# Four-layer block, last layer: part of ScalarE's and VectorE's feature work goes to GpSimd, and 72 expert tiles are spread over 82 blocks

## What is computed

```python
# L3 attention: 16 heads of 64 (1024 columns), a linear attention by features
def _feature_map(t):
    return jax.nn.elu(t) + 1.0
q = jnp.einsum('bsi,ihd->bshd', x, wq) + bq
k = jnp.einsum('bsi,ihd->bshd', x, wk) + bk
v = jnp.einsum('bsi,ihd->bshd', x, wv) + bv
Q = _feature_map(q)
K = _feature_map(k)
KV = jnp.einsum('bshd,bshd->bhd', K, v, precision=HI)
Ksum = jnp.sum(K, axis=1)
Z = 1.0 / (Q * Ksum[:, None, :, :] + EPS)
attn = Q * KV[:, None, :, :] * Z
out = jnp.einsum('bshd,hdo->bso', attn, wo) + bo
return jax.nn.gelu(out)

# L3 experts: the 2 best of 8 per token, hidden width 512
combine = jnp.sum(jax.nn.one_hot(top_idx, E) * routing_weights[..., None], axis=1)
for e in range(E):
    g = x @ gate_w[e].T
    u = x @ up_w[e].T
    y = jax.nn.silu(g) * u @ down_w[e].T
    out = out + combine[:, e:e + 1] * y

# the layer
xn = _layernorm(x, axis=-1)
x = x + _L3_attn_ref(xn, ...) + _L3_ffn_ref(xn, ...)
```

## Time and profile before

| | before |
|---|---|
| device time, median of 3 runs | 2943.32 us |
| span of the profiled execution (first to last instruction) | 2847.3 us |
| its device time beside the span | not listed; the runs shown took 2940.13 to 2945.33 us |
| PE busy over the span | 2442.7 us (86%) |
| DVE busy | 2005.6 us (70%) |
| ACT busy | 1823.8 us (64%) |
| POOL busy | 787.6 us (28%) |
| last layer's tile stage, from 2380.0 us | 332.5 us |
| from there to the first gather of the experts' results | 8.8 us |
| from the first gather (2721.3 us) to the end | 126.0 us |

### The profile page before, as it was taken

The page is one execution under the profiler, slowest core; times in us unless marked ns, Lnnn a source line. Parts: engine busy times, 40 slices in busy tenths (PEclk is TensorE's granted clock), DMA queues, the critical chain, the costliest instruction groups (busy, mean ns, idle before and its releaser), DMA issues. The chain is left out here.

```text
span 2847.3 us, 76648 instructions
## 1 busy us (share of the span) xinstructions
PE 2442.7 (86%) x30232; PEld 1812.5 (64%) x30232; DVE 2005.6 (70%) x5914; ACT 1823.8 (64%) x3779; POOL 787.6 (28%) x820
## 2 busy tenths in 40 slices
PE   6858999996889999999999899989996658999964
PEld 6745677774556666566656665666664547999943
DVE  5556544444568776877687677877775498999988
ACT  3334555553566666666666667666763488999997
POOL 3325100002133232323232223222222163111167
PEclk9959999997999999999999999999999689999998
DMA  6201355551000000000000000000000014666611
GB/s 211 38 16 40 115 158 160 155 156 56 11 17 15 4 17 17 15 4 17 17 15 4 17 17 17 9 10 13 14 13 7 1 45 156 203 195 202 192 42 51
DMA packets 104306, 175.17 MB, mean 62 GB/s; under 512 B 16273, under 2 KB 73745, under 8 KB 103825
## 3 DMA queue, kind: packets, MB, share of 16 engines
q1 hardware_dynamic: 94608, 153.20, 18.0%
q0 software_dynamic: 8192, 16.79, 2.0%
q10 hardware_dynamic: 1152, 0.27, 0.0%
HBM read 130.50 MB, written 26.74 MB: 55 GB/s over the span
## 5 line engine op out<-in xcount | busy, mean ns | idle before, releaser
L2014 POOL TENSOR_TENSOR l_rinv<-l_ssm,w_neg_half 128x8 f32<-128x8 f32 x128 | 210.2, 1642 | 551.8 <-DVE l_ssm L2305 551.7
L257 PE MATMUL bank<-l_kT,l_qT 32*128 32x128 f32 (+1 forms) x3072 | 355.0, 350 | 8.8 <-DVE l_qm L1382 7.2
L257 PE MATMUL bank<-l_qm,l_kT 32*128 32x128 f32 (+1 forms) x3072 | 350.7, 347 | 6.3 <-DVE l_qm L2215 6.3
L2045 ACT ACTIVATE l_probsT<-bank 128x768 f32<-128x768 f32 x256 | 208.5, 815 | 160.1 <-PE bank L257 159.3
L276 DVE TENSOR_REDUCE l_tops<-bank 128x2 f32<-128x256 f32 (+1 forms) x384 | 196.1, 511 | 119.9 <-PE bank L257 116.5
L2717 DVE RECIPROCAL l_rden<-l_den 128x256 f32<-128x256 f32 x128 | 223.8, 1748 | 30.0 <-ACT l_den L2628 29.4
L893 POOL DMA_INDIRECT back<-sorted_y,pos x128 | 125.6, 981 | 378.7 <-DMA sorted_y<-l_y_tile 347.8
L277 DVE TENSOR_REDUCE l_tops<-bank 128x2 f32<-128x512 f32 (+1 forms) x384 | 227.5, 592 | 0.0
L257 PEld LDWEIGHTS bank<-l_kT,l_qT 32*128 32x128 f32 x3072 | 205.8, 190 | 18.2 <-DVE l_qm L1382 9.3
L257 PEld LDWEIGHTS bank<-l_qm,l_kT 32*128 32x128 f32 x3072 | 202.9, 188 | 8.2 <-DVE l_qm L2215 8.1
L154 POOL TENSOR_TENSOR l_rstd<-l_var,w_neg_half 128x2 f32<-128x2 f32 (+1 forms) x56 | 42.6, 760 | 569.6 <-DVE l_var L149 556.8
(11 more groups left out here) (350 smaller groups left out, 6967.4 us busy)
## 6 DMA issues: line engine op xcount, KB each, us to landing
l_expert<-in_experts SPq DMA_DIRECT2D x72, 768.0 KB, 4.1
l_expert<-in_experts SPq DMA_DIRECT2D x72, 578.0 KB, 3.5
l_x_tile<-sorted_x SPq DMA_DIRECT2D x144, 64.0 KB, 4.1
sorted_y<-l_y_tile SPq DMA_DIRECT2D x144, 64.0 KB, 3.7
l_v_half<-l_v SPq DMA_DIRECT2D x32, 264.0 KB, 3.2
sorted_x<-x_all SPq DMA_DIRECT2D x18, 256.0 KB, 3.9
l_v_half<-l_v SPq DMA_DIRECT2D x32, 132.0 KB, 3.2
l_x<-in_x SPq DMA_DIRECT2D x8, 256.0 KB, 5.0
```

Source lines behind the costliest of these rows:

```text
L257: lasts.append(pe.matmul(bank[:, at:at + n * P], lhs[:, c * P:(c + 1) * P], rhs[:, x0 * P:(x0 + n) * P], start=False, stop=(i == 1), skip_ ...
L2014: pool.tensor_tensor(rinv[:, i, :], ssm[:, i, :], g.neg_half[:, 0:LH], ALU.pow).then_inc(rinv_ready[l], 1)
L2045: Bt.took(act.activation(probsT[:, (j // 2) % 2, 2 * (j % 2):2 * (j % 2) + 2, :], two[:, :, 0:AW], ACT.Exp), rd, use)
```

## The change

For the blocks that lie beside the tiles, from n = 26 to n = 107, and for these alone:

- POOL takes the exponentials less one and plus one (`part`), two instructions over 512 elements. ACT's `minus_one` and `plus_one` are left out there.
- ACT makes relu(q + bias) from the query bank in one more instruction, `q_pos`, and POOL adds the exponential's part to it (`query_features`). DVE's instruction for the query features is left out. max(t + 1, exp(-relu(-t))) is the same as relu(t) + exp(-relu(-t)).
- The query bank is free once ACT has read it, and no longer waits for DVE.

The 72 tiles lie beside 82 blocks instead of 72. Ten of these blocks, n = 26, 34, 42, 50, 58, 67, 75, 83, 91 and 99, have no tile. `C0` moves from 100 to 110, and the 32 chunks of the combination are spread over 17 turns instead of 27.

```diff
-    A0 = 26
-    C0, CL = A0 + TILES + 2, NB - 1 - (A0 + TILES + 2)
+    A0, AL = 26, 82
+    C0, CL = A0 + AL + 2, NB - 1 - (A0 + AL + 2)
+    P0, P1 = A0, A0 + AL
+    def on_pool(n):
+        return P0 <= n < P1
...
-            no_tiles = n <= A0 - 4 or n > A0 + TILES
+            no_tiles = n <= A0 - 4 or n > A0 + AL
...
-        def tile(n):
-            return n if 0 <= n < TILES else None
+        TILE_AT = {n: t for n in range(A0, A0 + AL) for t in share(TILES, AL, n - A0)}
+        TILE_AT.update({A0 - 1: -1, A0 + AL: TILES, A0 + AL + 1: TILES + 1})
+        def tile(n, k=0):
+            t = TILE_AT[n] + k if n in TILE_AT else None
+            return t if t is not None and 0 <= t < TILES else None
...
+        def wait_q_bank(eng, n):
+            if on_pool(n):
+                eng.wait_ge(q_pos_ready, so_far(n, True))
+            else:
+                eng.wait_ge(q_used, n + 1)
... PE, project
-                    pe.wait_ge(q_used, held_until[n] + 1)
+                    wait_q_bank(pe, held_until[n])
... POOL
+            def part(n):
+                k = so_far(n, True)
+                pool.wait_ge(raw_ready, k)
+                ch(pool.tensor_scalar(exp_less[:, n % 2, :, :], exp_raw[:, n % 2, :, :], 1.0, -1.0, ALU.mult, ALU.add))
+                pool.tensor_scalar(exp_part[:, n % 3, :, :], exp_less[:, n % 2, :, :], 1.0, 1.0, ALU.mult,
+                                   ALU.add).then_inc(pool_exp_ready, 1)
+            def query_features(n):
+                k = so_far(n, True)
+                pool.wait_ge(q_pos_ready, k)
+                pool.wait_ge(pool_exp_ready, k)
+                pool.wait_ge(attn_ready, n - 2)
+                pool.wait_ge(q_used, n)
+                pool.tensor_tensor(q_feat[:, n % 3, :], q_pos[:, n % 2, :], exp_part[:, n % 3, 1, :],
+                                   ALU.add).then_inc(q_used, 1)
             for n in range(NB + 2):
+                if on_pool(n):
+                    part(n)
+                    query_features(n)
                 if n >= EARLY + 2:
                     attend(n - 2)
... ACT, at the end of negatives
+                if on_pool(n):
+                    if on_pool(n - 2):
+                        act.wait_ge(q_used, n - 1)
+                    act.activation(q_pos[:, n % 2, :], Q[n][:, 0:S], ACT.Relu, bias=w["bq3"][:, m:m + 1]).then_inc(q_pos_ready, 1)
... ACT, exponential and the loop
+                if on_pool(n - 2):
+                    act.wait_ge(pool_exp_ready, so_far(n - 2, True))
...
-                if n < NB:
+                if n < NB and not on_pool(n):
                     minus_one(n)
                     plus_one(n)
... DVE, features
-                dve.wait_ge(exp_ready, n + 1)
+                wait_exp(dve, n)
...
+                if not on_pool(n):
+                    if n == P1:
+                        dve.wait_ge(q_used, n)
                     dve.scalar_tensor_tensor(out=q_feat[:, n % 3, :], in0=Q[n][:, 0:S], scalar=bq_one[:, m:m + 1],
                                              in1=exp_part[:, n % 3, 1, :], op0=ALU.add, op1=ALU.max).then_inc(q_used, 1)
```

More of the change, by code:

```diff
@@ L2371, in layer3, with so_far @@
     SG = CH // 4
-    A0 = 26
-    C0, CL = A0 + TILES + 2, NB - 1 - (A0 + TILES + 2)
+    A0, AL = 26, 82
[3 more added lines that the diff above has]
+        return P0 <= n < P1
+    def so_far(n, pooled):
+        return sum(1 for k in range(n + 1) if on_pool(k) == pooled)
     with ExitStack() as ctx:
@@ L2394, in layer3 @@
         kv_junk = sb("kv_junk", [P, S])
+        q_pos = sb("q_pos", [P, 2, S])
         k_sum = sb("k_sum", [P, FB])
@@ L2422, in layer3 @@
         exp_ready = sem("exp_ready")
+        raw_ready = sem("raw_ready")
+        pool_exp_ready = sem("pool_exp_ready")
+        q_pos_ready = sem("q_pos_ready")
         k_ready = sem("k_ready")
@@ L2532, in _ @@
                     project(n)
[L2533 to L2539, removed]
+                if tile(n, 1) is not None:
+                    turn_tile(tile(n, 1))
+                if tile(n) is not None:
+                    gate_up(tile(n))
+                if tile(n, -1) is not None:
+                    down(tile(n, -1))
                 if n >= 3:
@@ L2606, in exponential @@
                 ch.wait(made["neg"])
-                made["raw"] = ch.mark(act.activation(exp_raw[:, n % 2, :, :], neg_part[:, n % 2, :, :], ACT.Exp, scale=-1.0))
+                if on_pool(n - 2):
+                    act.wait_ge(pool_exp_ready, so_far(n - 2, True))
+                raw = act.activation(exp_raw[:, n % 2, :, :], neg_part[:, n % 2, :, :], ACT.Exp, scale=-1.0)
+                if on_pool(n):
+                    raw.then_inc(raw_ready, 1)
+                else:
+                    made["raw"] = ch.mark(raw)
             def tanh(t):
@@ L2643, in _ @@
             for n in range(NB + 7):
-                t = n - A0
-                if tile(t - 2) is not None:
-                    take_y(t - 2)
+                if tile(n, -2) is not None:
+                    take_y(tile(n, -2))
                 if n < NB:
@@ L2652, in _ @@
                     experts_weight(c)
-                if tile(t + 1) is not None:
-                    take_x(t + 1)
+                if tile(n, 1) is not None:
+                    take_x(tile(n, 1))
                 if n < NB:
                     exponential(n)
-                if tile(t) is not None:
-                    tanh(t)
-                if n < NB:
+                if tile(n) is not None:
+                    tanh(tile(n))
+                if n < NB and not on_pool(n):
                     minus_one(n)
@@ L2781, in _ @@
                     attend(n - 2)
-                if tile(n - A0) is not None:
-                    gate(n - A0)
+                if tile(n) is not None:
+                    gate(tile(n))
                 for c in share(CH, CL, n - C0 - 2):
                     experts_part(c)
-                if tile(n - A0) is not None:
-                    hidden(n - A0)
+                if tile(n) is not None:
+                    hidden(tile(n))
         s.next_layer()
```

8 lines of the change are left out of this document (6 added, 2 removed).

## The result

The changed kernel takes 2975.9 us (median; 2974.5 to 2976.7) against 2941.7 for the kernel before on the same chip: ratio 1.012, 95% interval 1.0106 to 1.0135, or +34 us. I had forecast slower, by 21.5 us. The direction was right. The ten blocks without a tile cost more than forecast in two ways: they were longer themselves (41.5 us against 34), and the blocks behind five of them ran at half of TensorE's clock for a while (9.8 us), for which the forecast had nothing.

A forecast was written before the change was run, and what follows sets the result against it. PE was taken to bound the tile stage at 4.53 us a block and POOL the stretch behind. Tile stage +31.5 us, behind it -10, gave +21.5 on 2943.3: about 2965 us, range 2949 to 2977.

The forecast's parts named there:

- PE bounds the tile stage, relief for ACT and DVE is worth nothing: Tile stage: PE's 4.53 us a block hides ACT and DVE; relieving them returns at most 2.5 us.
- The 2.5 us of lateness: Tile stage: time from DVE and ACT being late once in eight blocks, the most their relief could return.
- A gap costs DVE's chain, not PE's 1.74 us: Blocks without a tile: PE waits for DVE's features, so each takes 3.0 us instead of PE's own 1.74.
- At n % 8 = 3 the gap is 3.8: Five of the ten tile-less blocks: two more DVE instructions ahead make each 3.8 us.
- I had costed the collisions at nothing: DVE's gelu beside POOL: 2 us of waiting in eight blocks, hidden by 4.5 us slack; 20 us if uncovered.
- the term of the gaps in the sum: Ten blocks without a tile: 5 x 3.0 + 5 x 3.8 = 34 us; tile stage 364 against 332.5, +31.5 us.
- the prediction's own third sign: Tile stage: prediction is wrong if blocks with a tile take more than 4.7 us, through POOL or SBUF collisions.
- Behind the tiles -10 us: First gather to end: ten `attend` fewer on POOL (7.4 us) and 3.0 us of waits lost; -7 to -12.
- rival 1: Behind the tiles: ACT, not POOL, sets the end, saving 36 us; time 2939, down to 2927; chance 5%.
- rival 3: Beside the tiles: POOL becomes the bound at 4.5 us a block; time 2970 to 2975; chance 15%.
- rival 2: Blocks without a tile cost PE only 1.8 to 2.2 us each; +6.5 us, time 2950; chance 17%.

The follow-up runs named there:

- e2: Kernel before plus GpSimd's part of the change alone, 72 tiles beside 72 blocks, no gaps: ratio 0.9997 against the kernel before.
- e6: Changed kernel with ACT's `q_pos` moved behind the exponential and tanh of its turn: ratio 1.0083 against the kernel before.
- e8: Changed kernel with the gelu's square y*y replaced by o*y, o read from PSUM without its bias: ratio 1.0112 against the kernel before.
- e5: Changed kernel run again unedited, on a chip where the kernel before takes 2945 us: ratio 1.0110 against the kernel before.
- e9: Kernel before with every second attention product from block 100 on made by DVE instead of POOL: ratio 1.0001 against the kernel before.
- e10: Kernel before with all 28 attention products from block 100 on made by DVE instead of POOL: ratio 1.0009 against the kernel before.
- e3: Spreading alone: 72 tiles beside 82 blocks, ACT and DVE keeping all their work: ratio 1.0112 against the kernel before.
- e7: Changed kernel with DVE's gelu square at n % 8 = 3 moved behind the features of that turn: ratio 1.0067 against the kernel before.
- e11: Changed kernel with three repairs: nine gaps moved to n % 8 = 7, `q_pos` behind tanh, square behind features: ratio 1.0060 against the kernel before.
- e4: Changed kernel with nine of the ten gaps moved to n % 8 = 7 (26 stays): ratio 1.0076 against the kernel before.
- e12: Changed kernel with four extra unused PE matmuls in each of the five gaps at n % 8 = 3: ratio 1.0099 against the kernel before.
- e1: The kernel before, run again unedited: ratio 0.9995, 2854 us.

## Why the prediction came out too small

- *PE bounds the tile stage, relief for ACT and DVE is worth nothing*: right. 4.53 us stayed the commonest distance, and e2 is the direct proof. The 2.5 us of lateness that the relief was to return did not come back either (e2: 334.8 us).
- *A gap costs DVE's chain, not PE's 1.74 us*: right as a mechanism (e6 moves it by exactly the 0.36 us of `q_pos`), at 3.31 where I had 3.0. Part of the rest is hand-over, which I had left out: in the gap at block 83 PE starts 0.1 us behind DVE's last end, ACT's negatives 0.2 us behind PE's, and keys times values waits 0.43 and not 0.31 us for the key features.
- *At n % 8 = 3 the gap is 3.8*: 4.62. The rest is the 0.3 above and the collision of the square, 0.5 (e8). I had costed the collisions at nothing, since DVE's slack would hide them. In blocks with a tile it does: the five gelu lines take 3.65 us in eight blocks where they took 1.98 before, +1.7 us, where I had estimated 2. But the gap is the one place where DVE has no slack, and one of those instructions stands in it. The Trainium skill, SBUF — State Buffer, section Who interferes with whom, says that a DVE instruction with two SBUF inputs contends with a GpSimd one that reads SBUF, and one with at most one SBUF input (outside its 2-port modes) does not. The traces agree: beside POOL up to 0.95 us with two inputs (e5), 0.43 at most with one (e8).
- **The step that failed** is the term of the gaps in the sum, "Without one PE idles until 1.7 and then projects: 3.0 us", with "Together 5 x 3.0 + 5 x 3.8 = 34 us" and 4.53 us for every tile block behind. It priced idling of PE at its length alone and put the clock behind it at nothing, without a reason. The runs showed in its place: behind 2.1 us of idling PE's clock fell to half, five times, at 1.6 to 1.7 us and once 3.05, 9.8 us in all; and the gaps took 41.5 us and not 34. The 9.8 us are 60% of what the forecast of the stage lacked (47.7 against 31.5), the gaps' own length the rest. By the prediction's own third sign, over 4.7 us for blocks with a tile, it was wrong too: they average 4.72, from the clock and not from POOL. My rows of before could have warned me: the earlier trace rows has PEclk 0.87 in the stretch where PE idles half of the time, and 1.00 beside the tiles.
- *Behind the tiles -10 us*: -11.9, within the range, but in part by luck. The term takes POOL's work off the 126.0 us as if POOL had held them, and in the kernel before it did not (e9, e10). The figure fits because the new stretch comes out at the sum of POOL's work: 113.7 us in rival 1, 114.1 measured.
- *POOL as bound (rival 3)*: no. 0.62 and 0.73 us each make 2.9 us a block with the waits, and POOL is busy for 57% of the stage, not 75%. *ACT sets the end (rival 1)*: no; behind the tiles it is now busy for 72 of 107.6 us. *Cheap gaps (rival 2)*: no; even the three repairs left 3.55 us.

## What to carry to other kernels

Where one engine fills a stretch, thinning the work of the others there buys nothing, and making room beside it (here blocks without a tile) costs what the slowest dependency chain takes, not what the bound engine has to do. Put such a hole where no extra instruction of another engine sits in that chain, and count what an idle TensorE pays behind it: after 2.1 us of idling in these runs mostly half the clock for 3 us, after 1.4 us nothing. An engine that looks fullest in a balanced stretch need not hold it: take work off it in a run before counting on the gain.

## What the runs showed of the hardware

- A one-input POOL instruction over 128x512 took 0.62 us, the two-input one 1.27 at the same size and 0.73 at half of it.
- A DVE product with both inputs in SBUF took up to 0.95 us beside POOL's instructions and 0.42 without; with one input in PSUM always 0.42 to 0.43, beside POOL or not.
- TensorE's clock fell behind one idle stretch of PE where PE was full otherwise, in 5 of 5 gaps of the changed kernel, again in e5 (2.10 us idle, and 0.37 more in the same gap), in 5 of 5 of e3 (2.05 to 2.11), in 4 of 5 of e6 (2.10) and in 4 of 5 of e8 (1.58 and 0.38 more). It never fell behind 0.8 us (the gaps at n % 8 = 2), 1.12 (e7), 1.41 (e11) or 1.75 (e3, twice). So the length of the idling does not settle it alone. Ahead of the tiles, where the clock was moving anyway, it is less clear still: behind block 26 full clock after 2.37 to 3.25 us of idling (e6, e7, e11), half after 2.17 to 3.70 (the changed kernel, e3, e4, e5, e8, e12). What else decides stays open.
- The kernel before took 2854 us on one chip and 2945 on each of three others, with a mean granted clock of 0.953 and 0.937 to 0.939; the last layer's tile stage took the same time on both kinds to within 2 us (332.2 us in e1, 334.0 in e9, whose edit starts behind it).
